# Fewer initial loads, and gathers that wait for ScalarE, in an xDeepFM forward pass

## The reference

```python
emb = tables[feat_idx, sparse]                     # (512, 26, 32): a gather
linear_out = lin_sparse_w[feat_idx, sparse].sum(-1) + dense @ lin_dense_w
for w, bb in ((conv1_w, conv1_b), (conv2_w, conv2_b)):
    hp = einsum('bhd,bmd->bhmd', xk, x0).reshape(-1, h * M, E)
    xn = sigmoid(einsum('oi,bid->bod', w, hp) + bb[None, :, None])
    xk, keep = xn[:, :64], xn[:, 64:]
cin_out = concat(keeps).sum(-1) @ cin_w + cin_b
h3 = tanh(tanh(tanh(concat(emb, dense) @ W1 + b1) @ W2 + b2) @ W3 + b3)
return linear_out + cin_out + h3 @ deep_w + deep_b + bias
```

## Time and profile before

| What | Value |
|---|---|
| three runs | 533.96, 538.4, 538.56 us (median 538.4) |
| the profiled execution's own time | 535.66 us |
| its span, first to last instruction | 533.8 us |
| TensorE busy | 469.8 us, 88% |
| VectorE, ScalarE, GpSimd busy | 325.5, 202.6, 273.5 us |
| mean granted clock of TensorE | 0.974 |

### The profile page before, as it was taken

One profiled execution on the slowest core, in us unless ns is written; L12 is line 12 of the kernel. 1 busy time (PEld: TensorE's weight loads), 2 busy tenths in 40 slices (PEclk: granted clock), 3 DMA queues, 4 the chain that ended last, 5 costly groups with the idle time before them and its releaser, 6 DMA issues.

```text
span 533.8 us, 5489 instructions
## 1 busy us (share of the span) xinstructions
PE 469.8 (88%) x1946; PEld 196.7 (37%) x1946; DVE 325.5 (61%) x349; ACT 202.6 (38%) x346; POOL 273.5 (51%) x240
## 2 busy tenths in 40 slices
PE   1055968899999999999999999989999999999998
PEld 0032413233333333323333333333333332588685
DVE  3142643677777777776868677777777778462121
ACT  2156135263544435263635354535444313111111
POOL 6725747184738364655647585856263706490000
PEclk9996979899999999999999999999999999999999
DMA  5110110001000001010000202011000200020000
GB/s 155 23 18 8 15 20 5 14 2 14 7 11 8 9 10 48 9 48 12 6 8 1 56 2 56 16 41 41 8 24 0 73 7 1 29 90 0 1 1 0
DMA packets 22766, 11.98 MB, mean 22 GB/s; under 512 B 17922, under 2 KB 20588, under 8 KB 22740
## 3 DMA queue, kind: packets, MB, share of 16 engines
q1 hardware_dynamic: 19156, 9.88, 7.0%
q0 software_dynamic: 3584, 1.76, 2.7%
HBM read 9.92 MB, written 0.00 MB: 19 GB/s over the span
## 4 chain that ended last, share of the span: by engine, by line
PE 73%; DVE 7%; issue 7%; ACT 6%; another core or an unknown queue 2%; POOL 1%; DMA 1%; SPq 1%; DVEq 0%; ACTq 0%
PE l2out L334 32%; PE l1out L309 13%; PE spread L324 13%; PE l1out L402 6%; PE sums L402 6%; DVE prod L599 6%; PE sums L299 2%; ACT xk L457 2%; ACT sq_hi L448 1%; POOL emb L244 1%; DVE x L532 1%; ACT res L459 1%; ACT sq L447 1%; ACT x L435 1%
## 5 line engine op out<-in xcount | busy, mean ns | idle before, releaser
L599 DVE TENSOR_TENSOR prod<-spread,xk 128x1024 f32<-128x1024 f32 x208 | 252.1, 1219 | 125.0 <-PE spread L324 107.6
L334 PE MATMUL l2out<-prod,w_sb 128*64 128x512 f32 x832 | 229.6, 631 | 25.0 <-DVE prod L599 19.6
L255 POOL TENSOR_TENSOR sq_lo<-sq,sq_hi 117x512 fp32r<-117x512 f32 x90 | 113.5, 1283 | 142.8 <-ACT sq_hi L448 142.8
L244 POOL DMA_INDIRECT emb<-in_table,rows x112 | 108.1, 965 | 33.8 <-issue 30.6
L324 PE MATMUL spread<-x,sel_sb 58*128 58x512 f32 x416 | 105.2, 504 | 0.0
L324 PEld LDWEIGHTS spread<-x,sel_sb 58*128 58x128 f32 x416 | 39.6, 187 | 171.8 <-issue 164.9
L457 ACT ACTIVATE xk<-l1out,small_sb 64x512 f32<-64x512 f32 x64 | 43.6, 682 | 152.6 <-PE l1out L309 132.7
L447 ACT ACTIVATE sq<-sums 117x512 f32<-117x512 f32 x96 | 57.7, 601 | 47.5 <-PE sums L299 43.0
L334 PEld LDWEIGHTS l2out<-prod,w_sb 128*64 128x64 f32 x832 | 41.7, 136 | 87.7 <-DVE prod L599 52.0
L448 ACT ACTIVATE sq_hi<-sums 117x512 fp32r<-117x512 f32 x96 | 58.0, 604 | 0.0
L299 PE MATMUL sums<-x,sel_sb 58*117 58x512 f32 x96 | 21.2, 436 | 27.6 <-issue 18.9
(11 more groups left out here) (76 smaller groups left out, 298.9 us busy)
## 6 DMA issues: line engine op xcount, KB each, us to landing
wpiece<-in_mlp SPq DMA_DIRECT2D x11, 512.0 KB
emb<-in_table,rows POOLq DMA_INDIRECT x112
raw<-emb SPq DMA_DIRECT2D x96, 16.0 KB
raw<-emb SPq DMA_DIRECT2D x64, 2.0 KB
sel_f<-in_sel SPq DMA_DIRECT2D x1, 832.0 KB
w_sb<-in_w SPq DMA_DIRECT2D x1, 416.0 KB
wpiece<-in_mlp SPq DMA_DIRECT2D x1, 308.0 KB
w1a_sb<-in_w1a SPq DMA_DIRECT2D x1, 175.5 KB
```

Source lines behind the costliest of these rows:

```text
L244: pool.indirect_dma_start(out=emb[0:n, i, j, :], out_offset=None, in_=table, in_offset=bass.IndirectOffsetOnAxis(ap=rows[0:n, i, j:j + 1], ...
L255: nc.gpsimd.tensor_tensor(sq_lo[0:UK, u, c, :], sq[0:UK, s % SQR, :], sq_hi[0:UK, u, c, :].bitcast(F32), ALU.subtract).then_inc(lo_done, 1)
L334: mm = nc.tensor.matmul(l2out[c * HALF:(c + 1) * HALF, :], w2_sb[:, t, :], prod[r % 2][:, c, :], start=(t == 0), stop=(t == T2 - 1))
L599: nc.vector.tensor_tensor(prod[r % 2][:, :, :].rearrange("p c n -> p (c n)"), spread[r % 2][:, :, :].rearrange("p c n -> p (c n)"), xk[i % ...
```

## The change

Ten initial loads become five. Indices and bases arrive in one load (`idx_sb` has a second plane). Layer 1's three parts, the first selector, the biases and `ind` arrive in one load, `const_sb`, 1316 numbers wide on 128 partitions; those names become views of it, and all who waited for one of the parts now wait for `const_in`. The second selector and layer 2's weights keep loads of their own. And in `gather(i)` GpSimd waits for `x_hi_done` to reach i - 1, that is, until `x_high` of pair i - 2 has run.

```diff
-            sp.dma_start(idx_sb[:, :, :], idx).then_inc(idx_in, 16)
-            sp.dma_start(base_sb[:, :, :], idx_base).then_inc(base_in, 16)
-            sp.dma_start(w1a_sb[:, :, :], w1a).then_inc(w1_in, 16)
-            sp.dma_start(w1b_sb[:, :, :], w1b).then_inc(w1_in, 16)
-            sp.dma_start(fix_sb[:, :, :], w1_fix).then_inc(w1_in, 16)
-            sp.dma_start(sel1_f[:, :, :], sel1).then_inc(sel_in, 16)
+            sp.dma_start(idx_sb[:, :, :, :], idx).then_inc(idx_in, 16)
+            sp.dma_start(const_sb[:, :], const).then_inc(const_in, 16)
             sp.dma_start(sel2_f[:, :, :], sel2).then_inc(sel_in, 16)
-            sp.dma_start(small_sb[:, :], small).then_inc(small_in, 16)
             sp.dma_start(w2_sb[:, :, :], w2).then_inc(w2_in, 16)
             for i in range(RX):
                 lay_out(i)
-            sp.dma_start(ind_sb[:, :, :], ind).then_inc(ind_in, 16)
...
             def gather(i):
+
+                if i >= 2:
+                    pool.wait_ge(x_hi_done, i - 1)
                 if i >= GSEM:
                     pool.wait_ge(rows_in[i % GSEM], ROWS * (i // GSEM))
...
-            act.wait_ge(sel_in, 32)
+            act.wait_ge(const_in, 16)
             nc.scalar.activation(sel1_sb[:, :, :], sel1_f[:, :, :], ACT.Copy).then_inc(sel_done, 1)
+            act.wait_ge(sel_in, 16)
             nc.scalar.activation(sel2_sb[:, :, :], sel2_f[:, :, :], ACT.Copy).then_inc(sel_done, 1)
             x_high(0)
-            act.wait_ge(small_in, 16)
             act.wait_ge(w1_step, 5)
...
-            dve.wait_ge(base_in, 16)
             dve.wait_ge(idx_step, 3)
-            nc.vector.tensor_tensor(rows[:, :, :], clamped[:, :, :], base_sb[:, :, :], ALU.add).then_inc(idx_step, 2)
+            nc.vector.tensor_tensor(rows[:, :, :], clamped[:, :, :], idx_sb[:, 1, :, :], ALU.add).then_inc(idx_step, 2)
...
-            dve.wait_ge(w1_in, 48)
+            dve.wait_ge(const_in, 16)
```

More of the change, by code:

```diff
@@ L42, with build @@
 C_B1, C_B2, C_B3, C_DEEP, C_CB1, C_CB2, C_CIN1, C_CIN2, C_AUX, C_END = 0, 8, 12, 14, 16, 17, 18, 20, 22, 23
-def build(nc, idx, idx_base, table, dense_t, w1a, w1b, w1_fix, w2, mlp1, mlp2, mlp3, small, sel1, sel2, ind, out):
+SMALL_AT = 0
+IND_AT = SMALL_AT + C_END
+W1A_AT = IND_AT + 3 * PB
+W1B_AT = W1A_AT + UT * P
+FIX_AT = W1B_AT + UT * P
+SEL1_AT = FIX_AT + UT * M
+CONST = SEL1_AT + NPR
+def build(nc, idx, table, dense_t, const, w2, mlp1, mlp2, mlp3, sel2, out):
     with ExitStack() as ctx:
@@ L65, in sem @@
             return ctx.enter_context(nc.semaphore(name))
-        small_sb = sb("small_sb", [P, C_END])
-        ind_sb = sb("ind_sb", [P, 3, PB])
+        const_sb = sb("const_sb", [P, CONST])
+        small_sb = const_sb[:, SMALL_AT:IND_AT]
+        ind_sb = const_sb[:, IND_AT:W1A_AT].rearrange("p (k b) -> p k b", b=PB)
+        w1a_sb = const_sb[0:UK, W1A_AT:W1B_AT].rearrange("p (u o) -> p u o", u=UT)
+        w1b_sb = const_sb[0:UK, W1B_AT:FIX_AT].rearrange("p (u o) -> p u o", u=UT)
+        fix_sb = const_sb[0:UK, FIX_AT:SEL1_AT].rearrange("p (u m) -> p u m", u=UT)
+        sel1_f = const_sb[:, SEL1_AT:CONST].rearrange("p (u k) -> p u k", u=UT)
         aux = sb("aux", [P, B])
@@ L88, in build @@
         xt_lo = sb("xt_lo", [P, K1, B], F32R, at_a + K1 * B * 4)
-        w1a_sb = sb("w1a_sb", [UK, UT, P], F32, at_a)
-        w1b_sb = sb("w1b_sb", [UK, UT, P], F32, at_a + UT * P * 4)
         at_c = space(0)
@@ L105, in build @@
         xt = sb("xt", [P, K1, B])
-        idx_sb = sb("idx_sb", [P, NPAIR, GJ], I32)
-        base_sb = sb("base_sb", [P, NPAIR, GJ], I32)
+        idx_sb = sb("idx_sb", [P, 2, NPAIR, GJ], I32)
         wrap = sb("wrap", [P, NPAIR, GJ])
@@ L111, in build @@
         rows = sb("rows", [P, NPAIR, GJ], U32)
-        fix_sb = sb("fix_sb", [UK, UT, M])
         end_c = top[0]
-        sel1_f = sb("sel1_f", [P, UT, UK], F32, at_c)
         sel2_f = sb("sel2_f", [P, T2, P], F32, at_prod)
@@ L135, in build @@
         row_ps = l2out
-        idx_in, base_in, small_in, ind_in = sem("idx_in"), sem("base_in"), sem("small_in"), sem("ind_in")
-        w1_in, w2_in, sel_in, dense_in = sem("w1_in"), sem("w2_in"), sem("sel_in"), sem("dense_in")
+        idx_in, const_in, w2_in = sem("idx_in"), sem("const_in"), sem("w2_in")
+        sel_in, dense_in = sem("sel_in"), sem("dense_in")
         piece_in = [sem("piece_in0"), sem("piece_in1")]
@@ L336, in main @@
                 mm.then_inc(main_done, 1)
-            pe.wait_ge(w1_in, 48)
+            pe.wait_ge(const_in, 16)
             pe.wait_ge(w1_step, 2)
@@ L378, in _ @@
                             layer1(i + 2, 0)
-            pe.wait_ge(ind_in, 16)
             pe.wait_ge(lin_step, 1)
@@ L555, in _ @@
             dve.wait_ge(idx_in, 16)
-            nc.vector.tensor_scalar(wrap[:, :, :], idx_sb[:, :, :], 0.0, float(V), ALU.is_lt, ALU.mult)\
+            nc.vector.tensor_scalar(wrap[:, :, :], idx_sb[:, 0, :, :], 0.0, float(V), ALU.is_lt, ALU.mult)\
               .then_inc(idx_step, 1)
             dve.wait_ge(idx_step, 1)
-            nc.vector.tensor_tensor(inside[:, :, :], idx_sb[:, :, :], wrap[:, :, :], ALU.add).then_inc(idx_step, 1)
+            nc.vector.tensor_tensor(inside[:, :, :], idx_sb[:, 0, :, :], wrap[:, :, :], ALU.add).then_inc(idx_step, 1)
             dve.wait_ge(idx_step, 2)
@@ L701 @@
     mlp1[K1 - 1, :K1_LAST] = w1[NG * GM * E:]
+    base = np.broadcast_to(feature[:, None, :] * V, idx.shape)
+    rowwise = lambda w: tiles(w).reshape(UK, -1)
+    const = np.zeros((P, CONST), f32)
+    const[:, SMALL_AT:IND_AT] = small
+    const[:, IND_AT:W1A_AT] = ind.reshape(P, -1)
+    const[:UK, W1A_AT:W1B_AT] = rowwise(conv1[:, first, second].T)
+    const[:UK, W1B_AT:FIX_AT] = rowwise(conv1[:, second, first].T)
+    const[:UK, FIX_AT:SEL1_AT] = rowwise(fix)
+    const[:, SEL1_AT:CONST] = sel1
     arrays = {
-        "idx": np.ascontiguousarray(idx.astype(np.int32)),
-        "idx_base": np.ascontiguousarray(np.broadcast_to(feature[:, None, :] * V, (P, NPAIR, GJ)).astype(np.int32)),
+        "idx": np.ascontiguousarray(np.stack([idx, base], axis=1).astype(np.int32)),
         "table": np.concatenate([a(L0_rec_tables), a(L0_rec_lin_sparse_w)[:, :, None]], axis=2).reshape(M * V, ROW),
         "dense_t": np.ascontiguousarray(a(r_dense).T),
-        "w1a": tiles(conv1[:, first, second].T),
-        "w1b": tiles(conv1[:, second, first].T),
-        "w1_fix": tiles(fix),
+        "const": const,
         "w2": np.ascontiguousarray(conv2.transpose(3, 1, 2, 0).reshape(P, T2, HALF)),
         "mlp1": mlp1.reshape(K1 * P, D1), "mlp2": a(L0_rec_W2), "mlp3": a(L0_rec_W3),
-        "small": small,
-        "sel1": np.ascontiguousarray(sel1.reshape(P, UT, UK)),
         "sel2": np.ascontiguousarray(sel2.reshape(P, T2, P)),
-        "ind": ind,
     }
```

## The result

The changed kernel takes 538.78 us (median of 20 runs, 536.95 to 541.92), the kernel before 537.15 us (20 runs, 533.96 to 539.76). The ratio is 1.0041, with a 95% interval from 1.0025 to 1.0056: slower by 0.4%, some 2.2 us, small but clear of no change. The ratio is not that of the two medians, which lie 1.6 us apart (1.0030). The profiled execution has a span of 536.4 us, 2.6 us more than before.

The account below looks back on a forecast made before the run. TensorE with VectorE was taken to set the steady pace, 25.25 us a pair. Adding +0.1 us gave 535.8 us from the profiled execution and 538.5 from the median; the forecast was 537 us, between them, range 530 to 543.

Parts of the forecast that it names:

- the sum: Whole kernel: +0.1 us for the indices and 0 for everything else.
- the one on pairs 13 to 15: Gathers due at 294.74 us are held 2.0 us until `x_high(11)` has run, inside idle time; cost 0.
- The first rival: Near 65 us, holding parts pair 4's gathers from pair 3's layout; 5.0 to 6.9 us come back; chance 0.20.
- The third rival: Pair 2's held gathers begin with pair 1's layout, TensorE's signals get late: +6.9 us, 543 us; chance 0.05.
- The second rival: Pairs 6 to 12: held gathers end too late, delaying `low`; 543 or 560 us; chance 0.10.
- The meeting with `x_low`: Pair 7's held gathers begin beside VectorE's `x_low`, losing 0.4 us and leaving 2.0 us idle; cost 0.
- The start: Indices and bases in one load: +0.1 us; the merged constants load stays inside 12.2 us of cover: 0.
- The price of about 2.0 us: Initial loads: each transfer pays this besides its bytes, but loads overlap, so taking five away changes 0 us.

Follow-up runs that it names:

- `low` first: Kernel before with `low(i + 2)` ahead of `gather(i + 4)` on GpSimd, no hold: 528.89 us beside 536.38 (0.9846).

## Why the prediction was wrong

The forecast was 537 us, within 1% of before, and the measured 538.78 lies in its range. But it named +0.1 us as the sum, and the change costs 0.41%, with an interval that excludes zero.

- **The step that failed** is the one on pairs 13 to 15: "held by 2.0 us, again inside the idle time. Cost 0." The idle time was there (the run did not delay `low`: GpSimd still sat idle 2.76 us ahead of it, at 308.65 us), but the gathers of these pairs meet a layout, and moving them moved a moment of late signals onto the products. In place of cost 0 the hold of these three alone measured 3.1 us by the medians (0.57%, 0.36 to 0.79), and 2.4 us in the three steps of its trace, as in the changed kernel.
- **The rule behind it** was that a gather run costs something only through its own engine's queue. The trace of before showed otherwise at 65 us, and the prediction priced that stall as one event at one place. It did not look for smaller ones: the sigmoid at 304.15 us, 0.8 us late, was in the trace.
- **The first rival** had the mechanism of the stall right (gathers beside a layout) and so had the reason why the change would not touch it: ScalarE's sigmoid starts at 74.81 us after, 5.5 us late. Its price, 5.0 to 6.9 us, fits the 6.6 us that `low` first gains there, though by some luck: it counted the late signals alone, and the lower clock behind them has a part in the 6.6.
- **The third rival**, a second stall, was the right kind of loss at the wrong place. From 24 to 34 us nothing got late; the three late steps did.
- **The second rival** did not happen. The run of pair 7 starts at 145.79 and its last issue ends at 154.53 us, and GpSimd then waits 1.84 us where 2.0 were foreseen. The meeting with `x_low` was foreseen at 0.4 us; the first gather took 1.25 us where it took 0.93. The rule of the Trainium skill ("GPSIMD Engine Reference", Key points) and the trace agree on this. But not every such meeting costs: in the kernel before, `x_low` of 145.32 us ran beside gathers of 0.95 and 0.94 us, a meeting that the prediction names under this rival, though it counted only the one at 120.99 us. The held runs cost nothing: the hold of pairs 2 to 12 measured +0.2 us, inside the noise.
- **The start** went as worked out, a little worse: row numbers at 3.74 us instead of 3.48, `x_high` at 23.00 instead of 22.78 us. At 296 us the two traces are 0.07 us apart. The double load landed 2.1 us after its issue, where the single ones took 1.8 and 1.9 us. The price of about 2.0 us that the prediction took from the Trainium skill ("DMA: Bandwidth & Descriptors", Anatomy of one DMA) stands there for DMAs that GpSimd issues; these are SyncE's, and the three landings are near it all the same. Whether the merged loads cost anything beyond is open: +0.97 us alone and +0.69 us with `low` first are both inside the noise.
- **The size** is not settled to the microsecond: hold alone +3.5 us, both parts together +1.6 us by the medians and +2.2 by the ratio. The intervals overlap; no interplay of the two parts is shown.

## What to carry to other kernels

A wait that is "covered" on its own engine still moves everything that engine sends to the DMA queues; ask what those transfers will then run beside. Where one odd stall shows in a trace, look through the whole trace for its small relatives: results ready, receiver idle, and nothing running. And an order in which gathers and layouts don't meet was worth more here than a hold that ties gathers to another event: putting `low` ahead of the gathers took one swap and brought 7 us.

## What the runs showed of the hardware

TensorE's signals to ScalarE and VectorE arrive late, by 0.4 to 7.5 us, in stretches where indirect DMAs of GpSimd run beside layout DMAs of SyncE (ten of up to 128 pieces of 128 bytes, SBUF to SBUF). In the steady steps, where gathers and layouts follow each other, and with gathers issued 2.5 us behind a 512 KB load, none was late by more than 0.35 us. TensorE itself goes on starting matmuls meanwhile.

The late part is the signal and not the receiver. The trace also records when a semaphore is counted up. In the kernel before, six increments of TensorE belong to matmuls that end at 67.22, 68.23, 68.66, 68.89, 72.15 and 72.77 us, and they are recorded at 74.11, 74.17, 74.22, 74.26, 74.32 and 74.36 us: in the order of the matmuls, 0.04 to 0.06 us apart, as if they had queued. ScalarE starts at 74.14. The ends of matmuls in a trace are modelled, but where nothing is late the increment stands 0.01 to 0.02 us behind them (305.76 and 305.78 us, 306.42 and 306.43). Increments of VectorE in the same stretch stand within 0.02 us of the end of their operation, where they are recorded (63.33, 64.76 and 75.49 us).

Whether TensorE sends the signals late or they travel long, and why, no run here tells. It also stays open why the same meeting from 24 to 34 us made none late; of the layouts' parts (small pieces, few engines, count of DMAs) none was tried alone, nor was the length of the gather run.
